# First attention of a fused block on one core: three PSUM banks for exponentials and two for maxima, in place of two and three

## What is computed

```python
qkv = x @ Wqkv.T                      # b = 4, t = 1024, 16 heads of 8
dots = einsum('bhid,bhjd->bhij', q, k) * 8 ** -0.5
dots = where(triu(ones(t, t), 1), -inf, dots)
attn = softmax(dots)
out = einsum('bhij,bhjd->bhid', attn, v).transpose(...) @ Wout.T + bout
```

## Time and profile before

| | |
|---|---|
| median of 3 runs | 1891.05 us (1888.12 to 1892.08) |
| the profiled execution | 1890.3 us, with a span of 1888.3 us |
| loop over the groups of the first attention | from 358.19 us to about 898 us of the span |
| maxima of group 0, ahead of the loop | from 321 to 358 us |
| granted clock of PE, whole span | 0.93 of full |

### The profile page before, as it was taken

The page is one execution under the profiler, slowest core; times in us unless marked ns, Lnnn a source line. Parts: engine busy times, 40 slices in busy tenths (PEclk is TensorE's granted clock), DMA queues, the critical chain, the costliest instruction groups (busy, mean ns, idle before and its releaser), DMA issues. The chain is left out here.

```text
span 1888.3 us, 35242 instructions
## 1 busy us (share of the span) xinstructions
PE 1582.2 (84%) x12162; PEld 1091.1 (58%) x12167; DVE 1220.6 (65%) x2516; ACT 1056.5 (56%) x2103; POOL 693.1 (37%) x1145
## 2 busy tenths in 40 slices
PE   6997975899999999999799799346788888988774
PEld 5666863555555555553666577234566766667653
DVE  6633558887887888883664366465656777766544
ACT  2433432488888888887243244213566667667651
POOL 0786552111111111111058665352234545544342
PEclk9998997899999999999699899767899999999987
DMA  6122322011111111110413123200000000000000
GB/s 246 38 78 66 109 68 70 23 40 29 27 36 29 34 29 28 40 29 12 183 45 88 59 82 101 102 1 1 2 2 2 5 5 8 5 8 8 7 4 12
DMA packets 50494, 83.08 MB, mean 44 GB/s; under 512 B 11124, under 2 KB 35124, under 8 KB 49652
## 3 DMA queue, kind: packets, MB, share of 16 engines
q1 hardware_dynamic: 41236, 62.07, 11.4%
q0 software_dynamic: 9088, 18.76, 2.9%
HBM read 43.18 MB, written 31.22 MB: 39 GB/s over the span
## 5 line engine op out<-in xcount | busy, mean ns | idle before, releaser
L1920 DVE TENSOR_REDUCE z_parts<-z_pM 128x4 f32<-128x512 f32 x576 | 373.0, 685 | 95.9 <-PE z_pM L1658 92.1
L1835 ACT ACTIVATE z_Pr<-z_pE 128x512 f32<-128x512 f32 x576 | 322.2, 596 | 86.7 <-PE z_pE L1682 83.9
L1682 PE MATMUL z_pE<-z_QM,z_QK 128*128 128x512 f32 x576 | 251.0, 438 | 8.9 <-DMA z_QM<-z_Q 6.6
L2027 POOL TENSOR_SCALAR_AFFINE_SELECT z_Pr<-z_Pr 128x512 f32<-128x512 f32 x128 | 81.3, 635 | 481.2 <-ACT z_Pr L1835 481.2
L1658 PE MATMUL z_pM<-z_KM,z_Q 128*128 128x512 f32 x576 | 233.4, 410 | 1.5 <-DVE z_Q L1910 0.9
L1682 PEld LDWEIGHTS z_pE<-z_QM,z_QK 128*128 128x128 f32 x576 | 108.1, 188 | 159.3 <-ACT z_Pr L1835 91.5
L356 POOL DMA_INDIRECT slot_results<-m_yq,m_xq x156 | 153.7, 985 | 108.5 <-ACT m_yq L561 79.9
L332 POOL DMA_INDIRECT slot_rows<-m_XN,m_dest x128 | 129.3, 1010 | 94.5 <-DVE m_dest L650 59.2
L1695 PE MATMUL z_pO<-z_Pr,z_V 128*9 128x512 f32 (+3 forms) x1536 | 159.3, 488 | 0.1
L974 PE MATMUL f_gup<-s_wguT,f_xT 128*128 128x352 f32 x234 | 102.6, 523 | 33.8 <-DVE f_src L1281 18.9
L1658 PEld LDWEIGHTS z_pM<-z_KM,z_Q 128*128 128x128 f32 x576 | 109.4, 191 | 18.4 <-DVE z_parts L1920 3.2
(11 more groups left out here) (290 smaller groups left out, 3870.3 us busy)
## 6 DMA issues: line engine op xcount, KB each, us to landing
slot_rows<-in_c_pad SPq DMA_DIRECT2D x2, 5070.0 KB, 24.6
m_xq<-slot_rows SPq DMA_DIRECT2D x38, 260.0 KB
z_QM<-z_Q SPq DMA_DIRECT2D x128, 64.0 KB, 2.0
z_KM<-z_QK SPq DMA_DIRECT2D x60, 128.0 KB, 2.4
m_raw<-in_gu SPq DMA_DIRECT2D x2, 2048.0 KB, 8.7
m_XN<-slot_results SPq DMA_DIRECT2D x8, 512.0 KB
m_raw<-slot_results SPq DMA_DIRECT2D x8, 512.0 KB, 5.6
slot_results<-m_yq,m_xq POOLq DMA_INDIRECT x156
```

The lines of the kernel that those rows point to most:

```text
L1682: mm(pE[e % 2][:, :].rearrange("p (h c) -> p h c", h=4), QK[G % RING][:, kt * P:(kt + 1) * P], QM[half][:, :, q * P:(q + 1) * P], start=Tr ...
L1835: a.activation(Pr[j % 4][:, :, q * P:(q + 1) * P], pE[e % 2][:, :].rearrange("p (h c) -> p h c", h=4), ACT.Exp, scale=DH0 ** -0.5).then_in ...
L1920: v.tensor_reduce(parts[:, qt, kb, :], pM[n % 3][:, :].rearrange("p (h k) -> p h k", h=4), AX.X, ALU.max).then_inc(maxed, 1)
L2027: g_.affine_select(blk, blk, [[0, 4], [1, P]], ALU.is_ge, 0.0, base=0, channel_multiplier=-1).then_inc(selected, 1)
```

## The change

The six banks of the two passes are dealt out anew: `pE` gets three and `pM` two. The exponential's matmul e now waits for the exponential e - 3 in place of e - 2. The maximum's matmul n, and the mask's copy for it, wait for the reduction n - 2 in place of n - 3. No instruction is added or taken away, and none moves in its engine's list.

```diff
-        pE = [s.ps(f"pE{u}", [P, 512]) for u in range(2)]
-        pM = [s.ps(f"pM{u}", [P, 512]) for u in range(3)]
+        pE = [s.ps(f"pE{u}", [P, 512]) for u in range(3)]
+        pM = [s.ps(f"pM{u}", [P, 512]) for u in range(2)]
...
-                    need(pe, maxed, NM * G + n - 2)
+                    need(pe, maxed, NM * G + n - 1)
...
-                    last = mm(pM[n % 3][:, :]...
+                    last = mm(pM[n % 2][:, :]...
...
-                    need(pe, exp_done, NE * G + e - 1)
-                    mm(pE[e % 2][:, :]...
+                    need(pe, exp_done, NE * G + e - 2)
+                    mm(pE[e % 3][:, :]...
...
-                    act.wait_ge(maxed, NM * G + n - 2)
-                    a.activation(pM[n % 3][:, :], after_query[:, :], ACT.Copy).then_inc(filled, 1)
+                    act.wait_ge(maxed, NM * G + n - 1)
+                    a.activation(pM[n % 2][:, :], after_query[:, :], ACT.Copy).then_inc(filled, 1)
...
-                        a.activation(Pr[j % 4][:, :, q * P:(q + 1) * P], pE[e % 2][:, :]...
+                        a.activation(Pr[j % 4][:, :, q * P:(q + 1) * P], pE[e % 3][:, :]...
...
-                    v.tensor_reduce(parts[:, qt, kb, :], pM[n % 3][:, :]...
+                    v.tensor_reduce(parts[:, qt, kb, :], pM[n % 2][:, :]...
```

More of the change, by code:

```diff
@@ L1653, in max_unit @@
                         need(pe, k_masked[G % 2], 64 * (G // 2 + 1))
-                    need(pe, maxed, NM * G + n - 2)
+                    need(pe, maxed, NM * G + n - 1)
                     if G and kb == qt:
                         pe.wait_ge(filled, len(DIAG) * (G - 1) + DIAG.index(n) + 1)
-                    last = mm(pM[n % 3][:, :].rearrange("p (h k) -> p h k", h=4), Q[G % 2][:, qt * P:(qt + 1) * P],
+                    last = mm(pM[n % 2][:, :].rearrange("p (h k) -> p h k", h=4), Q[G % 2][:, qt * P:(qt + 1) * P],
                               KM[G % 2][:, :, kb * P:(kb + 1) * P], start=(G == 0 or kb < qt), stop=(G > 0 or kb < qt), skip_group_check=True)
                     if G == 0 and kb == qt:
-                        last = mm(pM[n % 3][:, :], identb[:, :], after_query[:, :], start=False, stop=True, skip_group_check=True)
+                        last = mm(pM[n % 2][:, :], identb[:, :], after_query[:, :], start=False, stop=True, skip_group_check=True)
                     last.then_inc(sm_ready, 1)
@@ L1680, in exp_unit @@
                         need(pe, v_kept, NW)
-                    need(pe, exp_done, NE * G + e - 1)
-                    mm(pE[e % 2][:, :].rearrange("p (h c) -> p h c", h=4), QK[G % RING][:, kt * P:(kt + 1) * P],
+                    need(pe, exp_done, NE * G + e - 2)
+                    mm(pE[e % 3][:, :].rearrange("p (h c) -> p h c", h=4), QK[G % RING][:, kt * P:(kt + 1) * P],
                        QM[half][:, :, q * P:(q + 1) * P], start=True, stop=True, skip_group_check=True).then_inc(st_ready, 1)
@@ L1834, in main @@
                             need(act, pv_done, NJ * G + j - 3)
-                        a.activation(Pr[j % 4][:, :, q * P:(q + 1) * P], pE[e % 2][:, :].rearrange("p (h c) -> p h c", h=4),
+                        a.activation(Pr[j % 4][:, :, q * P:(q + 1) * P], pE[e % 3][:, :].rearrange("p (h c) -> p h c", h=4),
                                      ACT.Exp, scale=DH0 ** -0.5).then_inc(exp_done, 1)
@@ L1919, in max_unit @@
                         need(dve, mstep, 2 * G - 1 if n == 0 else 2 * G)
-                    v.tensor_reduce(parts[:, qt, kb, :], pM[n % 3][:, :].rearrange("p (h k) -> p h k", h=4),
+                    v.tensor_reduce(parts[:, qt, kb, :], pM[n % 2][:, :].rearrange("p (h k) -> p h k", h=4),
                                     AX.X, ALU.max).then_inc(maxed, 1)
```

## The result

The changed kernel takes 1923.37 us (median of 4 runs, 1920.87 to 1927.36), the kernel before 1889.59 us (4 runs, 1882.59 to 1892.08). The ratio is 1.0184, with a 95% interval of 1.0159 to 1.0209: 34.8 us slower by the ratio, between 30.0 and 39.5; the two medians differ by 33.8. Forecast were 1923.3 us, or +32.3. The profiled execution has a span of 1922.0 us against 1888.3.

A forecast was written before the change was run, and what follows sets the result against it. The prediction took PE, the matrix engine, to set the pace from 394 to 870 us. Its terms, 32.0 + 2.8 - 2.5 = +32.3 us, added to the median of 1891.05 gave 1923.3 us, range 1906 to 1945.

The forecast's parts named there:

- the 15 periods: Groups 1 to 15, two banks for the maxima: 2.13 us lost per period, +32.0 us in all.
- the 91.5 us of loads waiting for ACT: Exponentials' weight loads, 143 waits: a load behind `values` can't start earlier while PE works, so no real hold-up.
- Rival B: Whole kernel faster: DVE keeps up and only the gain stays, 1888.5 us, down to 1885; chance 0.04.
- The places: Steps of group 5 where PE's delay changes, walked one by one: 2.13 us a group in total.
- n = 2: Group 5: the mask copy, now held for reduction 0, makes the maximum's matmul 2 late by 0.19 us.
- E 10: The exponential's matmul 10 already waits some 0.35 us for spread queries; this swallows part of the delay, -0.10 us.
- Keep_maximum: On ACT behind the mask for n = 5: moves by 0.43 us, and the spread queries' DMAs with it.
- The copy of 5.97 us: Group 0: a small DVE copy for which PE waits anyway; some 1.4 us of earlier delay vanishes in it.
- Ahead of the loop: Maxima of group 0 with two banks: PE and DVE are level there; +2.8 us, between 0 and 4.
- Group 15: Exponentials alone, three banks: PE reaches `values` about 0.8 us sooner in three runs; -2.5 us, between 0 and -4.
- rival E: PE's clock: pauses grow until it falls to 1.2 GHz for a tenth of the time, 1974 us; chance 0.02.
- Rival D: ACT becomes the bound, as masks wait behind reductions and exponentials fall behind for good: 1948 us; chance 0.08.

The follow-up runs named there:

- pe_masks: The changed kernel without ACT's mask copies: PE adds the mask in all groups with a second matmul; ratio to the kernel before 1.0184.
- pe_masks_two_two: The edit of pe_masks made on two_two, so with two banks for the exponentials; ratio to the kernel before 1.0198.
- mask_wait: The kernel before, but only ACT's mask copy waits for the reduction n - 2; the matmuls wait as before; ratio 1.0158.
- matmul_wait: The kernel before, but only PE's maximum matmul waits for the reduction n - 2; the masks wait as before; ratio 1.0115.
- last_three: The kernel before, but group 15's exponentials take turns on three banks, two of pE and one of pM; ratio 0.9982.
- last_five: The kernel before, but group 15's exponentials take turns on five banks; ratio 0.9973. Its second version has turn_maximum and keep_maximum at e = 3, not 4: 0.9919.
- change_again: The changed kernel measured once more, with no edit; ratio to the kernel before 1.0206.
- two_two: The changed kernel with two exponential banks again and their wait as before, pM keeping two; ratio to the kernel before 1.0255.
- the two with the early turn: last_five and the changed kernel, each with turn_maximum(G, 1) and keep_maximum at e = 3 instead of 4; ratios to the kernel before 0.9919 and 1.0204.

## Why the prediction was right, step by step

In the trace of the changed kernel the stage is 38.8 us longer: 36.3 in the 15 periods, 4.9 ahead of them, 2.35 saved in group 15. Forecast were 32.0, 2.8 and 2.5. The whole moved by 33.7 us in the profiled executions, as 5.3 us less passed behind the stage, in work that the change does not touch. So by chance the total of 32.3 came closer than its terms. The intervals of the two measurements overlap from 32.5 to 39.5 us, and one term was clearly too small.

- **Reading the waits.** That the 91.5 us of loads waiting for ACT were cover was right as far as the runs go: in pe_masks and pe_masks_two_two, where no mask copies stand on ACT, two and three banks give the same period. Rival B falls by the measured time.
- **The places.** Each of the seven holds. How far M or E has fallen behind the kernel before in group 5, measured and forecast per step: n = 2 0.47 (0.19), n = 6 0.36 (0.34), E 10 -0.11 (-0.10), n = 12 0.35 (0.35), n = 20 and 22 0.68 (0.66), n = 25 0.35 (0.35), n = 31 0.36 (0.34); with rounding 2.47 (2.13).
- **The term that was mis-sized** is n = 2: 0.19 us in the sum, 0.47 measured, and 0.28 x 15 = 4.2 us. I took reduction 0 to end 1.60 us after E 0 (532.82 - 531.22), as before. In the changed kernel it starts 1.16 us after E 0 (548.08 - 546.92), not 0.92, and the mask for n = 2 waits for it. DVE's reductions of the group before are not late: reduction 35 ends 0.05 us ahead of E 0 before and 0.07 after. The delay comes over ACT and GpSimd, where I had not looked. At e = 34 stands the mask copy for n = 0, which now waits for reduction 34. Exponential 35 behind it ends 0.49 us after E 0, not 0.03, and GpSimd's causal select on its result moves with it. DVE's small instruction beside the select takes 0.37 us (L1930) before, and 0.63 (L1932, otherwise 0.19) in the changed kernel, each until just behind the select's end (531.95 and 548.12):

```profile
531.32 0.63 POOL L2027 TENSOR_SCALAR_AFFINE_SELECT z_Pr<-z_Pr 128x512 f32<-128x512 f32 x1 [1.98 <-ACT z_Pr L1835]
531.62 0.37 DVE L1930 CAST z_mw<-z_m 128x16 fp32r<-128x16 f32 x1
```

```profile
547.48 0.64 POOL L2027 TENSOR_SCALAR_AFFINE_SELECT z_Pr<-z_Pr 128x512 f32<-128x512 f32 x1 [2.45 <-ACT z_Pr L1835]
547.53 0.63 DVE L1932 TENSOR_TENSOR z_mw<-z_m,z_mw 128x16 fp32r<-128x16 f32 x1
```

Each trace has 64 of these small instructions. In the eleven traces with mask copies on ACT 15 of them take 0.36 us or more, and every one ends 0.03 to 0.06 us behind a GpSimd instruction; the others take 0.18 to 0.20, and none of them starts while GpSimd works. The copy of 5.97 us is one of the 15: it ends at 336.47, a GpSimd instruction of 8.84 us at 336.42. That the mask's wait starts this chain is shown by the two halves: reduction 0 starts 1.16 us after E 0 in mask_wait and 0.91 in matmul_wait. That GpSimd holds DVE is read from the rows; no run tests it alone.
- **Keep_maximum** moved by 0.73 us, not 0.43, from the same root, and E 10 by 0.72: it does follow one for one.
- **Ahead of the loop** the trace gives 4.9 us for 2.8. But this stretch varies by itself: in the five traces where PE waits for the reduction n - 3 (before, mask_wait, last_three and the two of last_five) it takes 37.0 to 39.6 us, in the eight where it waits for n - 2, 41.4 to 43.6. The means differ by 3.3 us (38.7 and 41.9), near the forecast.
- **Group 15** gave 2.35 us for 2.5. What I had not seen is that a late DMA for E 10 can cost this group more than the bank gives it, as in change_again.
- **The clock**, rival E, stayed full through all periods of the first trace, though PE was held at seven places in each. My reason against the rival, that no pause is over 0.6 us, was wrong: M 2 of the first round waits 1.44 us for its mask. In change_again the same pause took 1.45 us, and there the clock was at half from 364.52 to 371.34. The kernel before was at half too near that place (361.97 to 365.38), without such a pause, so this fall can't be laid to the banks. In none of the 13 traces did the clock fall from group 1 to group 14. The rule of the Trainium skill (page "TensorE: Matmul & The Clock Gate", section "A second HAM failure mode: psum-queue depth-cycling") finds no case in these groups: in the first trace, pauses of up to 1.5 us at E 10 and 0.35 at the maxima did not bring it about. In group 15 the clock fell in change_again within a pause of 2.09 us, and in matmul_wait 1.3 us behind one of 1.99, both for a DMA and not for a bank.
- **Rival D** falls too: ACT waits 82.5 us more, but it is busy 394.7 of 511 us, and its exponentials still wait 41.7 us for their matmuls (83 times, from 358 to 940 us).

Open: why 5.3 us less passed behind the stage in this one trace. Work that no edit touches varies as much elsewhere: behind the last exponential mask_wait takes 966.8 us and two_two 972.2, on one chip. Only one trace of the kernel before is to be had, and none on the other chips.

## What to carry to other kernels

A bank taken from a pair of engines that exchange work in turn costs where the work bunches, not on the average: here DVE had 88 us to spare in 476, and two banks still held PE at the third unit of each run. Look for every instruction that inherits the bank's wait; the mask copy on ACT cost more than the matmul's own wait, since it stood ahead of unrelated work in an in-order queue. And walk a loop twice round, on every engine, before you multiply: here the mask of the last step delayed an exponential, that one GpSimd's select, and the select DVE's first reduction of the next round. Where a resource is idle in the last round, lend it there, as last_five does.

## Not expected

E 10 of group 15 waited for its DMA until 8.3 us after the group's start in most traces (7.4 in the two with the early turn), but 9.6 and 9.5 us in two (change_again, matmul_wait). In both the granted clock was then at its lower level for part of what followed, and in change_again the stretch from E 10 to the last exponential took 20.1 us, against 17.5 in the changed kernel's first trace. So in change_again a DMA that landed 1.3 us late, with the fall of the clock beside it, cost this group 3.9 us.
